# Three graph layers on one core: last projection begun between node tiles, query spread inside it, maxima as rows under the mask

## The reference

```
h = relu(layernorm(x));  x = x + gcn(h, W0, b0)
h = relu(layernorm(x))
def rgat(x, W, q, k, b, heads):            # W: 3 relations, 768 x 768
    xr = einsum('nd,rdf->rnf', x, W)
    oi, oj = xr[etype, dst], xr[etype, src]
    alpha = leaky_relu(oi @ q + oj @ k, 0.2)
    e = exp(alpha - segment_max(alpha, dst)[dst])
    a = e / (segment_sum(e, dst)[dst] + 1e-16)
    return segment_sum(a * oj, dst) + b
x = x + rgat(elu(rgat(h, W1, q1, k1, b1, 4)), W2, q2, k2, b2, 1)
```

## Time and profile before

| | us |
|---|---|
| median of 3 runs (1753.17 to 1764.15) | 1756.65 |
| the profiled execution, its own time | 1749.84 |
| span of its trace | 1748.0 |

### The profile page before, as it was taken

How to read it: one execution, slowest core, us unless ns; L and a number is a source line. 1 busy time by engine, 2 the same in 40 slices (tenths; PEclk the granted TensorE clock), 3 DMA queues, 4 the chain that set the end, 5 groups by cost and what they waited for, 6 DMA issues and landing times.

```text
span 1748.0 us, 25342 instructions
## 1 busy us (share of the span) xinstructions
PE 1506.7 (86%) x6330; PEld 879.2 (50%) x6330; DVE 926.9 (53%) x2169; ACT 220.2 (13%) x530; POOL 1016.0 (58%) x1112
## 2 busy tenths in 40 slices
PE   5989999989866995999699999864997998899996
PEld 2545555545554553566454455433554655455553
DVE  8576722333434877888677777603533345222322
ACT  1545200000000110011000023320110111000000
POOL 1598266665434767775167777515656662666663
PEclk9988999999966997889799999965998999899999
DMA  8201588888720231111188888720231111888887
GB/s 289 113 19 38 188 265 270 268 297 268 228 66 11 56 101 28 38 37 40 65 265 269 263 257 246 223 71 1 56 109 39 38 47 49 280 263 271 263 260 263
DMA packets 86808, 271.76 MB, mean 155 GB/s; under 512 B 32156, under 2 KB 32531, under 8 KB 86743
## 3 DMA queue, kind: packets, MB, share of 16 engines
q0 software_dynamic: 51072, 199.44, 37.7%
q1 hardware_dynamic: 34807, 65.62, 10.5%
q10 hardware_dynamic: 864, 5.90, 0.9%
HBM read 239.28 MB, written 31.62 MB: 155 GB/s over the span
## 4 chain that ended last, share of the span: by engine, by line
PE 57%; issue 14%; DMA 11%; POOL 8%; DVE 8%; DVEq 1%; ACT 1%; another core or an unknown queue 0%; POOLq 0%; SPq 0%; PEldq 0%; ACTq 0%
PE ps L1293 12%; PE ps L1226 9%; DMA ring<-keys,idxr 8%; PE ps L1253 7%; PE ps L1295 6%; PE ps L1296 6%; POOL ring L488 6%; PE ps L1124 5%; DVE zw L962 2%; PE ps L1167 2%; PE ps L1170 2%; PE ps L1187 2%; PE ps L1045 2%; PE ps L1074 1%; PE ps L1087 1%
## 5 line engine op out<-in xcount | busy, mean ns | idle before, releaser
L1253 PE MATMUL ps<-wreg,hT 128*128 128x384 f32 x1440 | 490.0, 503 | 7.4 <-PEq L1246 6.7
L488 POOL DMA_INDIRECT ring<-keys,idxr x312 | 331.1, 1061 | 220.8 <-DMA ring<-keys,idxr 95.3
L459 POOL DMA_INDIRECT ring<-rows,idxr x304 | 311.5, 1025 | 201.7 <-issue 66.6
L1253 PEld LDWEIGHTS ps<-wreg,hT 128*128 128x128 f32 x1440 | 282.2, 197 | 203.9 <-issue 26.7
L1293 PE MATMUL ps<-ring,zw 128*128 x664 | 229.1, 497 | 22.0 <-issue 14.9
L1226 PE MATMUL ps<-ring,zw 128*128 x664 | 223.9, 493 | 21.4 <-DVE zw L851 12.4
L957 DVE TENSOR_TENSOR hn<-hn,al 128x1024 f32 (+1 forms) x166 | 137.6, 829 | 181.7 <-POOL al L506 139.8
L459 POOL DMA_INDIRECT ring<-rows,idx x152 | 145.7, 958 | 116.2 <-PE ps L1226 65.6
L1293 PEld LDWEIGHTS ps<-ring,zw 128*128 128x128 f32 x664 | 122.5, 191 | 123.0 <-issue 53.5
L1226 PEld LDWEIGHTS ps<-ring,zw 128*128 128x128 f32 x664 | 123.8, 191 | 116.0 <-issue 49.5
L1020 DVE TENSOR_TENSOR ring<-ring,al x166 | 159.3, 959 | 40.0 <-issue 19.8
(11 more groups left out here) (185 smaller groups left out, 1232.5 us busy)
## 6 DMA issues: line engine op xcount, KB each, us to landing
wreg<-in_L_gnn_W SPq DMA_DIRECT2D x11, 2304.0 KB, 9.5
rows<-stage SPq DMA_DIRECT2D x30, 386.0 KB
rows<-stage SPq DMA_DIRECT2D x30, 384.5 KB
stT<-targets_row ACTq DMA_DIRECT2D x6, 960.0 KB
ring<-keys,idxr POOLq DMA_INDIRECT x312
ring<-rows,idxr POOLq DMA_INDIRECT x304
rows<-stT SPq DMA_DIRECT2D x10, 384.0 KB, 2.9
xs<-in_x SPq DMA_DIRECT2D x3, 1152.0 KB, 13.5
```

Of the source, the lines that this page charges most:

```text
L459: nc.gpsimd.indirect_dma_start(ring[:, t % (2 * RING), 0:WIDTH[l]], None, rows[l], bass.IndirectOffsetOnAxis(idx[:, t:t + 1], 0)).then_inc ...
L488: nc.gpsimd.indirect_dma_start(kb[:, n % KSEMS, t % KB, 0:4], None, keys[l], bass.IndirectOffsetOnAxis(idxr[:, t:t + 1], 0)).then_inc(k_in ...
L1253: last = mm(ps[:, 2 * (nt % 2) + h, 0:HALF], hT[:, k, nt * P:(nt + 1) * P], wreg[:, r % 2, k, h * HALF:(h + 1) * HALF], start=(k == 0), st ...
```

## The change

- Layer two: KFLIGHT is 4 there and stays 2 in the last layer. KSEMS is 6 buffers of keys instead of 3; POOL still asks two batches ahead.
- PE projects the first half of relation 0's tile 0 and opens five of six banks before it waits for `q16` of layer two.
- ACT, not SP, starts the loads of the last layer's weights 0 and 1, after it has divided tiles 4 and 6 of layer two.
- PE projects tiles 0 and 1 of the last layer between the last node tiles of layer two.
- The query spread of the last layer goes to banks 4 and 5 and stands inside the projection, after tiles 2 to 5 (QUERY_AT). Its stride is 8 words, so three narrow MATMULs accumulate the three parts in PSUM; DVE no longer adds them.
- In the last layer the maxima are not spread to edges. DVE broadcasts a tile's maximum along a row block (`mcol`), PE transposes it (`mrow`), and in the sum of rows DVE computes mask + score - maximum for 128 targets (`less`), and ACT makes the weight by Exp, for each 128 edges. The Exp over all scores is gone there. PE waits for the gathered rows itself.

```diff
-KSEMS = 3
-KFLIGHT = 2
+KSEMS = 6
+AHEAD = 2
+KFLIGHT = {1: 4, 2: 2}
-BANK_Q, BANK_M = 2, 6
+BANK_Q, BANK_M = {1: 2, 2: 4}, 6
-SQ, SM = 32, 8
+SQ, SM = {1: 32, 2: 8}, 8
+QUERY_AT = {2: (0,), 3: (1, 2), 4: (3, 4, 5), 5: (6, 7, 8, 9)}
...
-                if l == 1:
-                    load_weights(2, 0)
-                    load_weights(2, 1)
...
+                if l == 2:
...
+                    with act.Fori(0, pairs) as i:
+                        for b in range(2):
+                            act.wait_ge(shifted, 2 * i + (b + 2))
+                            act.wait_ge(w_used[l], 2 * i + (b + 2 * RING - 1))
+                            nc.scalar.activation(weight[:, b, :], less[:, b, ds(i % 2, 1), :].rearrange("p a c -> p (a c)"), ACT.Exp).then_inc(w_in[l], 1)
...
+                        if j in (4, 6):
+                            r = (4, 6).index(j)
+                            act.dma_start(wreg[:, r, :, :], Wd[2][r].rearrange("(k p) n -> p k n", p=P)).then_inc(s_wb[2][r], 16)
...
+                    if l == 2:
+
+                        if j >= 2:
+                            dve.wait_ge(mrow_done, j - 1)
+                        V.tensor_scalar(mcol[:, j % 2, :], m.to_broadcast([P, P]), NEG / 2, None, ALU.max).then_inc(mrow_in, 1)
+                        return
...
+                def shifted_scores(i, j):
+
+                    dve.wait_ge(off_in, 2 * i + 2)
+                    dve.wait_ge(w_in[l], 2 * i + 2)
+                    dve.wait_ge(shifted, 2 * i + 1)
+                    for b in range(2):
+                        V.scalar_tensor_tensor(less[:, b, ds(i % 2, 1), :].rearrange("p a c -> p (a c)"), negm[:, ds(i % 2, 1), b, :].rearrange("p a c -> p (a c)"), al[:, ds(2 * i + b, 1)], mrow[:, j, :], ALU.add, ALU.subtract).then_inc(shifted, 1)
+                    for b in range(2):
+                        off(i + 1, b)
...
+            def max_row(j):
+
+                pe.wait_ge(mrow_in, j + 1)
+                nc.tensor.transpose(mrow[:, j, :], mcol[:, j % 2, :], ident[:, :]).then_inc(mrow_done, 1)
...
+                            if n >= 2 and l == 2:
+                                max_row(n - 2)
...
+                                if l == 2 and b == 0:
+                                    pe.wait_ge(g_in[l], 2 * i + (RING + 3))
```

More of the change, by code:

```diff
@@ L43 @@
 KBATCHES = 2 * NPAIR // KB
-KSEMS = 3
-KFLIGHT = 2
-assert KB % KFLIGHT == 0
+KSEMS = 6
+AHEAD = 2
+KFLIGHT = {1: 4, 2: 2}
+assert all(KB % n == 0 for n in KFLIGHT.values())
 assert KBATCHES * KB == 2 * NPAIR
@@ L223, in gnn_kernel @@
         m16 = sb("m16", [P, NT, 3, 4], BF16)
+        weight = zw[:, 0, :, 1, :]
+        less = zw[:, 1, :, 1:3, :]
+        mcol = zw[:, :, 0, 3, :]
+        mrow = psf[:, 5 * 512:5 * 512 + NT * P].rearrange("p (t c) -> p t c", t=NT)
         mx = sb("mx", [P, NT, 4])
@@ L286, in gnn_kernel @@
         qs_ready = sem("qs_ready")
-        k_in = {l: [sem(f"k_in{l}_{i}") for i in range(KFLIGHT)] for l in (1, 2)}
+        k_in = {l: [sem(f"k_in{l}_{i}") for i in range(KFLIGHT[l])] for l in (1, 2)}
         k_sum = {l: sem(f"k_sum{l}") for l in (1, 2)}
@@ L296, in gnn_kernel @@
         m16_ready = sem("m16_ready")
-        m_spread = {l: sem(f"m_spread{l}") for l in (1, 2)}
+        m_spread = sem("m_spread")
+        mrow_in, mrow_done = sem("mrow_in"), sem("mrow_done")
+        off_in, shifted = sem("off_in"), sem("shifted")
         al_ready, e_ready = sem("al_ready"), sem("e_ready")
@@ L510, in _ @@
                 pool.wait_ge(s_keys, 16 * R * l)
-                ask_keys(0)
-                ask_keys(1)
+                for n in range(AHEAD):
+                    ask_keys(n)
                 pool.wait_ge(qs_ready, l)
@@ L1196, in by_node, with project @@
                     nc.tensor.transpose(ps[:, QV_BANK[l], c:c + w], qkT[0:w, b * P:(b + 1) * P], ident[0:w, 0:w]).then_inc(qv_done, 1)
+            def project(l, r, nt, halves=(0, 1)):
+                for h in halves:
+                    pe.wait_ge(stage_in[l], r * (2 * NT) + (2 * nt + h + 1))
+                    for k in range(KT):
+                        last = mm(ps[:, 2 * (nt % 2) + h, 0:HALF], hT[:, k, nt * P:(nt + 1) * P], wreg[:, r % 2, k, h * HALF:(h + 1) * HALF], start=(k == 0), stop=(k == KT - 1))
+                    last.then_inc(p_ready, 1)
+            def max_row(j):
+                pe.wait_ge(mrow_in, j + 1)
+                nc.tensor.transpose(mrow[:, j, :], mcol[:, j % 2, :], ident[:, :]).then_inc(mrow_done, 1)
             def to_features(l, nt):
```

175 lines of the change are left out of this document (102 added, 73 removed).

## The result

The changed kernel takes 1789.93 us (median of 6 runs, 1782.45 to 1799.61), the kernel before 1756.53 us (6 runs). The ratio is 1.0195, 95% interval 1.0169 to 1.0221: 33 us slower. The forecast was 1756 us with a range up to 1778.

A forecast was written before the change was run, and what follows sets the result against it. PE's 86% busy hides stage limits; in the last layer POOL's scores and PE's projection end nearly together. Terms +1.5 - 13 + 2 + 18 - 4 - 5 = -0.5 us on 1749.84; forecast 1756 us against median 1756.65, range 1737 to 1778.

The forecast's parts named there:

- The late query (+18): Last layer's query spread inside the projection: queries ready at 1232 against 1214.36, +18 us (bounds +2 and +28).
- late query alone: Rival, last layer: full slow stretch beside the asks, no gain at its end, queries at 1242 or later; 1774 us, 15%.
- Four in flight (-13): Layer two's score stage: four key gathers in flight cut waits, so the stage ends about 13 us earlier (0 to 21).
- the first term (+1.5): Half a projection ahead of layer two's query spread: spread starts later, asks end sooner; +1.5 us (-3 to +5).
- The weights' loads (+2): Last layer's weights loaded during the first attention layer's sum, mostly free of charge; +2 us (0 to +7).
- The projections between the node tiles: Between layer two's last node tiles: extra projections fit gaps, full clock, keys leave earlier; -1 us (-3 to +6).
- The end of the score stage (-4): Last layer: row gathers start about 16.5 us after the last score, where it was 20.2; -4 us (0 to -6).
- The last sum (-5): Last sum of rows: ACT makes weights by Exp, residual step no longer holds weights back; -5 us (-17 to +8).
- ACT's turnaround: Rival, last sum of rows: ACT's waits and register work over 0.7 us a tile decide; 1789 us at 0.9, 13%.

The follow-up runs named there:

- after_pace: The changed kernel with a small POOL fill, waited for, after each of the first 24 key gathers of either attention layer; ratio 1.0021 to the kernel before (chip 15).
- own_pace: 'own' with a small POOL fill, waited for, after each of the first 24 key gathers of either attention layer; ratio 0.9896 to the kernel before (chip 15).
- ask_late: The changed kernel, but in the last layer POOL asks its first 24 keys only after PE has spread the queries; ratio 1.0217 to the kernel before.
- kf4_only: The kernel before with one edit: four key gathers in flight in layer two (six key buffers); ratio 0.9964 to the kernel before.
- own_sp: 'own' with last-layer weights loaded by SP after layer two's last gather and no half projection ahead of its query spread; ratio 0.9979 to the kernel before.
- kf4_pace: kf4_only with a POOL fill, waited for, after each of the first 24 gathers of either layer; ratio 0.9923 to the kernel before (chip 15).
- own: The changed kernel with the last layer's query spread alone ahead of projections, one MATMUL per product, no projection between node tiles; 1744.81 us, ratio 0.998 (chip 8).
- own_oldsum: 'own' with the last layer's maxima spread by PE, one Exp over all scores and DVE's one-hot weights put back; ratio 0.9997 to the kernel before.
- own_kf44: 'own' with four key gathers in flight in the last layer too, instead of two; ratio 1.0645 to the kernel before.
- own_kf41: 'own' with one key gather in flight in the last layer instead of two; one execution, 1937 us.
- own_beside: 'own' run again without edits, on chip 12 beside the kernel before; ratio 0.9892.

## Why the prediction was wrong

**The late query (+18) is the step that failed.** It was worked out from passes, projections and clock as if the slow stretch beside the asks stayed where it was. The parts were right: from the start of the projection of tile 2 to the first score I had 73 us (1157.3 to 1230); after_pace, without a crawl, has its first score 20.9 us later after the first gather than own_pace (59.4 and 38.5 us), which is the size of the term. ask_late, on a chip that does crawl, agrees: from the start of that projection to the end of DVE's part it took 69.6 us (1155.25 to 1224.80). Projections behind narrow work took 10.0 to 10.5 us, where I had 7.9 + 2.2 from the earlier trace rows. What I left out is the crawl's new place. From 1165.90 to 1263.50 there are 97.6 us, and 28 of them are the crawl in tile 0's loop. In the kernel before the same crawl cost 18 us but lay beside 32 us of gathers that POOL needed anyway. In the changed kernel everything else stands behind it: with tripled MATMULs, PE did two passes in 32 us where it had done some five in 28. I had written "up to 1199 the asks run beside new loop code as before" and added 2 us for it, without a working; 28 were due. My upper bound (+28, qs at 1242, rival "late query alone" with 15%) had the right mechanism, but gave the stretch 12 us; counted from the first gather it put the first score at 74 us, and it came at 86.9. Measured: 2.15%, 38 us for the whole of the late query, of which 21 are there without a crawl (after_pace against own_pace, on another chip) and the other 17 or so are left for the crawl.

**Four in flight (-13): right mechanism, too large.** Waits fell as I said and the stage shrank by 9 to 10 us (19.5 to 19.7 us for each of the first four batches, forecast 19.7). But PE stands still more beside the denser gathers: in the maxima spread of layer two it idles 14 to 17 us with no releaser in every kernel with four in flight on chips 8, 4 and 0 and in the changed kernel (2 us on chips 15 and 12), 4.7 before, and the first score came 3.6 us later in kf4_only alone. Net 6 us. In **the first term (+1.5)** the asks did end sooner, 31.2 us after the first one instead of 37.6, but the spread didn't: PE's idle time "issue" in it rose from 21.6 to 28.5 us, and from first gather to first score it took 59.9 us, 7.4 more than before. kf4_only has 3.6 of them with that one edit, and own_sp has all of them without the half projection.

**The weights' loads (+2):** 3 to 5 us of the stage by own_sp's chip, within the bounds; the trace pair's 8 (309.7 us from first row gather to first key gather, before 301.5) also holds the projections at its end and noise. The projections between the node tiles did what was said: the last query product ran at the full clock (2.75 us for the earlier trace rows's 5.28), and from the end of PE's last row product to the keys' write it took 26.0 us (1140.05 to 1166.00) instead of 28.2.

**The end of the score stage (-4):** 15.5 us from last score to first row gather, forecast about 16. Right.

**The last sum (-5): wrong sign on these chips.** 274.5 us in the changed kernel, 268 to 274 in the others with ACT's weights on chips 8, 4 and 0, 265 to 266 with DVE's. On chip 15 the sign is the one that was forecast: 237.4 to 238.7 us in the three kernels with ACT's weights, 242.5 in kf4_pace with DVE's. There PE's waits for ACT and its idle time "issue" all but vanish (0.9 us together in own_pace; 22.8 in 'own'). Waits in the changed kernel's last sum (total, times, longest):

```profile
DVE zw L1021 <- ACT zw L659: 81.7, 42, 4.0
...
PE ps L1367 <- issue: 15.8, 19, 2.6
...
PE ps L1367 <- ACT zw L659: 12.1, 16, 2.1
```

PE's 17.1 us of waits for DVE's weights turned into 12.1 for ACT's and 15.8 of "issue", which holds its own wait for the rows. ACT's turnaround isn't the bound (an Exp took 0.31 us, not 0.42), so that rival (13%) didn't happen. Why the sum is 2 to 8 us longer on the first chips, none of the runs isolates.

**The sum as it was and as it is:** -6 (four in flight), +6 with an uncertainty of 4 (loads and half projection: own_oldsum against kf4_only), -3 with an uncertainty of 5 (maxima as rows: own against own_oldsum), +38 with an uncertainty of 6 (late query) give +35; measured +33. That the four meet the total is no check: each is the step from one kernel to the next between the kernel before and the changed one. own_sp, which takes the second pair back from 'own', puts them at 0 with an uncertainty of 6. The forecast had -13, +3.5, -9 and +18 for the same four.

## What to carry to other kernels

Before narrow work is moved next to a run of back-to-back gathers on POOL, look in the trace for engines that idle with no releaser while POOL issues: that stretch is not a constant of the code, it stays with the gathers, and whatever stands behind it pays for it. With two in flight, keep long instructions (projections) beside them; with four even those crawled, and one in flight ended the crawl but cost some 180 us in all. A stage's waits for gathers are not all worth removing: taking them out of POOL's chain in the last layer cost 6.5%. And a ratio from one chip isn't evidence for a mechanism seen on another: the control there takes one run, on that very chip.

## What the hardware showed that I had not expected

- PE, and DVE too, can stand idle with no releaser while POOL issues gathers: 94 and 97 us in own_kf44, in steps of about 0.72 us. In the spreads of the last layer it began 3 to 9 us after the first gather and ended 1 to 5 us after the last of the 24. In own_kf44's projection it began 38 us after the first score and ended at 1416, and POOL's last 12 gathers, at 1.25 us each from 1417 on, ran without it on PE. No block of PE's code came between 1254 and 1425 there either; what PE lacks isn't shown.
- It differs between chips: 21.9 us of it on chip 8 and 4.6 on chip 12 for the same kernel, one trace each. On chip 12 the last sum of rows was also faster, 296 GB/s against 261 in the same stage.
- What the traces hold differs with it. The last layer's 168 key gathers should leave 2688 events of landing, 16 each. On the first chips there are 1727 in the kernel before, 1853 in 'own', 1584 in the changed kernel and 466 in own_kf44, but all 2688 in own_kf41, where nothing crawls; own_beside on chip 12 has all 2688 too. So events get lost where engines crawl. Whether the recording of events has a part in the crawl is a rival that no run here tests.
- A narrow loop with three MATMULs a product runs a pass at the same pace as one with one (1.8 us for 36 or 12 MATMULs) as long as nothing crawls; in the crawl it is the number of instructions that counts.
